# A selective scan with a quantised feed-forward: in slots with sums over states, TensorE does its other jobs first

## The reference, cut to what matters

```python
x = x + ssm(layernorm(x))     # 4 heads of 128 channels, 16 states each
x = x + ffn(layernorm(x))     # inner width 704

# ssm: xz = h @ in_proj.T; x, z = split; x = silu(conv4(x) + b)
#   dt_r, B, C = split(x_proj(x)); delta = softplus(dt_proj(dt_r) + dt_b)
def step(s, inp):                       # for every token, head, channel, state n
    d_t, u_t, B_t, C_t = inp
    s = s * exp(d_t * A[n]) + (d_t * u_t) * B_t[n]
    y_t = sum over n of s[n] * C_t[n]   # the sum over states
    return s, y_t
#   y = (y + x * D) * silu(z); out = y @ out_proj.T

# ffn: fp4(h) = h rounded in blocks of 16 values to the grid 0, .5, 1, 1.5, 2, 3, 4, 6
#   gate, up = fp4(h) @ fp4(w_gate).T, fp4(h) @ fp4(w_up).T
#   out = fp4(silu(gate) * up) @ fp4(w_down).T
```

## Time and profile before

| | |
|---|---|
| time, median of 3 runs | 4897.47 us (4894.6 to 4899.58) |
| the profiled execution: time, span | 4895.54 us, 4893.5 us |
| TensorE matmul busy | 4234.6 us (87%) |
| VectorE busy | 4549.8 us (93%) |
| ScalarE busy | 3509.2 us (72%) |
| POOL busy | 3429.2 us (70%) |
| mean granted TensorE clock | 0.988 of full |
| spreads L904 | 690.1 us, 393.5 us idle before |
| sums L919 (`ybank`, `cross`) | 1003.4 and 1003.1 us, side by side |
| up projection L993 | 357.8 us |
| gate product L797 | 132.5 us, 210.4 us idle before |

### The profile page before, as it was taken

One profiled execution on the slowest core, in us unless ns is written; L12 is line 12 of the kernel. 1 busy time (PEld: TensorE's weight loads), 2 busy tenths in 40 slices (PEclk: granted clock), 3 DMA queues, 4 the chain that ended last, 5 costly groups with the idle time before them and its releaser, 6 DMA issues. The chain is left out here.

```text
span 4893.5 us, 64416 instructions
## 1 busy us (share of the span) xinstructions
PE 4234.6 (87%) x18927; PEld 1986.9 (41%) x19244; DVE 4549.8 (93%) x6828; ACT 3509.2 (72%) x5783; POOL 3429.2 (70%) x2321
## 2 busy tenths in 40 slices
PE   4788888888888888888898888888888888888887
PEld 1234444444444444444444444444444444444434
DVE  6999999999999999999999999999999999999994
ACT  3777777677777777777777777777777777777763
POOL 4777777777776777777777677777777677677763
PEclk8999999999999999999999999999999999999999
DMA  2333333333333333333333333333333333333330
GB/s 89 140 135 123 127 129 125 121 132 126 120 133 124 123 129 129 123 123 134 119 127 131 122 126 127 127 123 130 126 120 133 124 123 129 129 123 123 129 117 19
DMA packets 211138, 600.59 MB, mean 123 GB/s; under 512 B 25446, under 2 KB 76774, under 8 KB 210790
## 3 DMA queue, kind: packets, MB, share of 16 engines
q1 hardware_dynamic: 209088, 594.30, 35.6%
q10 hardware_dynamic: 1702, 2.16, 0.2%
HBM read 575.39 MB, written 20.97 MB: 122 GB/s over the span
## 5 line engine op out<-in xcount | busy, mean ns | idle before, releaser
L629 POOL TENSOR_TENSOR prod<-state,cs 128x1024 f32<-128x1024 f32 x1024 | 2416.5, 2360 | 1320.8 <-DVE state L852 1295.2
L440 ACT ACTIVATE decay<-delta,aneg 128x512 f32<-128x512 f32 x2048 | 1432.6, 717 | 925.3 <-DVE state L852 916.7
L840 DVE TENSOR_TENSOR db<-db,du 128x512 f32<-128x512 f32 x2048 | 1392.0, 680 | 56.7 <-PE db L904 55.5
L852 DVE TENSOR_TENSOR_SCAN state<-decay,carry,db 128x512 f32<-128x512 f32 x1024 | 1292.4, 1262 | 0.0
L852 DVE TENSOR_TENSOR_SCAN state<-decay,db 128x512 f32<-128x512 f32 x1024 | 1232.6, 1204 | 0.0
L904 PE MATMUL db<-pieces,sel 128*128 128x512 bf16 x1798 | 690.1, 386 | 393.5 <-DVE state L852 384.6
L919 PE MATMUL ybank<-prod,ident 64*64 64x512 f32 x4096 | 1003.4, 608 | 28.0 <-DVE hh L790 27.0
L919 PE MATMUL cross<-prod,ident 64*64 64x512 f32 x4096 | 1003.1, 609 | 0.0
L904 PEld LDWEIGHTS db<-pieces,sel 128*128 128x128 bf16 x2048 | 197.8, 97 | 1039.9 <-DVE state L852 809.0
L919 PEld LDWEIGHTS ybank<-prod,ident 64*64 64x64 f32 x4096 | 255.8, 134 | 455.1 <-issue 417.8
L1040 PE MATMUL bank_a<-wd,ht 128*128 128x256 f32 x1536 | 406.0, 389 | 3.2 <-DVE state L852 2.0
(11 more groups left out here) (124 smaller groups left out, 6399.6 us busy)
## 6 DMA issues: line engine op xcount, KB each, us to landing
cs<-c_rows SPq DMA_DIRECT2D x1024, 512.0 KB, 3.6
xin<-in_hidden SPq DMA_DIRECT2D x128, 128.0 KB, 3.6
xres<-in_hidden SPq DMA_DIRECT2D x128, 128.0 KB, 3.4
out_x<-ot SPq DMA_DIRECT2D x128, 128.0 KB, 3.6
c_rows<-xdbl SPq DMA_DIRECT2D x128, 32.0 KB, 3.6
win<-in_win_t SPq DMA_DIRECT2D x1, 1024.0 KB, 10.6
state<-in_w_gate ACTq DMA_DIRECT2D x1, 704.0 KB
state<-in_w_up ACTq DMA_DIRECT2D x1, 704.0 KB
```

The lines of the kernel that those rows point to most:

```text
L440: act.activation(decay[:, g.val() % RING, :], delta[:, gu % 2, :], ACT.Exp, scale=aneg[:, gu % HEADS, gn:gn + 1]).then_inc(decayed, 1)
L629: pool.tensor_tensor(prod[:, r, :, :], state[:, 2 * p:2 * p + 2, :], cs[:, c, :, :], ALU.mult).then_inc(weighted, 1)
L840: dve.tensor_tensor(t[:, :], t[:, :], du[:, gu % 2, :], ALU.mult).then_inc(db_done, 1)
L852: dve.tensor_tensor_scan(state[:, n, :], decay[:, g.val() % RING, :], db[DB_BANK[g.k % TRIP]][:, :], start, ALU.mult, ALU.add).then_inc(sc ...
```

## The change

In TensorE's `step` the call of `side` moves ahead of the loop over the groups of sums. The spread stays first. In slots without sums nothing changes.

```diff
                 if g.within(STEPS):
                     spread_b(b, g)
+                side(b, u, due)
                 for slot, pairs in SUMS.items():
                     if w := due("scan", slot):
                         sum_up(w, pairs)
-                side(b, u, due)
```

## The result

The changed kernel takes 4950.43 us (median of four runs, 4949.61 to 4951.24), the kernel before 4898.52 us on the same occasions. The ratio is 1.0105, 95% interval 1.0088 to 1.0123: slower, by some 52 us. Forecast were 4943 us and a range of 4917 to 4968.

A forecast was written before the change was run, and what follows sets the result against it. VectorE sets the pace (busy 4549.8 of 4893.5 us), TensorE close behind, two chains nearly tied at L787. 2.88 us a trip over 15.3 trips, +44 us, and some 2 us for the first six units gave 4943 us, range 4917 to 4968.

The forecast's parts named there:

- Slot 0: TensorE's L963 waits for `xdbl` without the sums as cover; VectorE's product late by 0.80 us (units 1-3), 0.44 us (units 5-7).
- Slot 3: L993 goes 1.88 us ahead, but L797 then waits for the SiLU and L787 for L516; slot 3 itself saves 0.08 us.
- unit 0: First unit of a trip: `mid` early, slot 3's spread 0.42 us earlier, with slot 3's 0.08 a gain of 0.50 us.
- the middle of 0.62: Unit 4, slot 0: VectorE's product taken as 0.62 us late, between 0.80 and 0.44; unit loss 0.50 us.
- less up to 0.08: Late units, slot 3: deduction from L516's delay, 0.44 - 0.08 less up to 0.08, giving 0.32 us for units 5 to 7.
- +2 us for the first six units: Units before post jobs exist (from unit 6 on): only slot 0 counts, some 2 us.
- Slot 8: Last third of the down projection (L1040) ahead of pairs 0 and 1: value 0, bounds -0.2 to +0.2 us a unit.
- A: Rival, faster: L787 not tied to TensorE's slot 3, only VectorE's own chain counts; -36 us, 4861 us; chance 0.08.
- D: Rival, naive hope: L797's wait shrinks to the SiLU's limit, no slot 0 delay; -100 us, 4797 us; chance 0.02.
- B: Rival, no change: L963's wait shorter than read, units 1 to 7 lose no more than unit 0's 0.50 us; 4897 us; chance 0.05.
- C: Rival, slower: the new idle piece drops TensorE's clock in one unit of eight; 89 us on top, 5032 us; chance 0.04.

The follow-up runs named there:

- e2: Kernel before the change, with side jobs ahead of the sums in slot 0 alone: 4963.39 us, ratio 1.0141.
- e4: Changed kernel, with ScalarE's slot 15 decay behind the two copies of pbank so that `xdbl` ends earlier: 4883.83 us, ratio 0.9982 to the kernel before.
- e1: Kernel before the change, with side jobs ahead of the sums in slot 3 alone: 4886.22 us, ratio 0.9984.
- e5: Kernel before, with side jobs first in slot 3 alone and ScalarE's third decay of slot 6 moved to slot 7, behind L516: 4819.51 us, ratio 0.9841.
- e3: Kernel before the change, with side jobs ahead of the sums in slot 8 alone: 4898.23 us, ratio 1.0006.
- e9: Kernel before, with slots 3 and 8 turned, L1007 alone ahead of slot 0's sums, first SiLU ahead of centring, L516 behind one decay: 4761.87 us, ratio 0.9729.

## Why the prediction was right

**Slot 0.** Forecast was a chain of 3.06 us from the end of `xdbl` to L840; it is 1366.03 - 1362.92 = 3.11 us. The product is late by 0.82 us in units 1 to 3 (forecast 0.80) and 0.50 us in units 5 to 7 (0.44). That this wait is the cause is shown by e2, which has it alone and loses 69 us, and by e4, which halves it and ends 11 us below the kernel before.

**Slot 3.** L797's wait of 0.73 us, for the SiLU, is as forecast, and the SiLU still ends 2.92 us after scan 2. Slot 3 takes 1371.36 - 1367.97 = 3.39 us, as forecast. L787's 0.84 us was forecast as 0.7 to 0.9. e1 and e5 show that the tie at L787 is real.

**Size.** A trip costs 3.5 us; forecast 2.88. Units 1 to 3 grew by 0.70 us (0.64), unit 4 by 0.63 (0.50), units 5 to 7 by 0.44 (0.32); unit 0 shrank by 0.50 us as forecast. Three terms were mis-sized. In unit 4 the product is 0.70 us late, not the middle of 0.62. The step from the spread to L840 was 0.05 us longer: in e4, where slot 1's spread has its record, it is 0.53 us and not 0.47. And in units 4 to 7 the "less up to 0.08" for TensorE being the later one at slot 3 doesn't exist: in late units its spread follows scan 2 by 0.07 us before the change too.

These 0.6 us a trip are 9 us. The span grew by 54.2 us, where the forecast had 46: 52.2 in the fifteen trips behind the first, 4.7 behind the last scan, and -2.7 up to the end of the first trip. The forecast had +2 us for the first six units and no term for what lies behind the last scan (last section). These two misses, -4.7 and +4.7 us, cancel by luck.

**Slot 8** was priced at nothing, and e3 measures nothing.

**The rivals.** A and D (4861 and 4797 us) fail because L787 is tied to TensorE's slot 3: what they promised is what e5 reaches only with L516 out of the way. B fails in units 1 to 3. C, a clock that falls at the new idle piece, does not happen; this is the window that was shown of before, in the changed kernel:

```profile
1300.00:2400.00 1100.00, 958.91 (x4344) 451.55 (x4420) 1037.65 (x1567) 799.70 (x1326) 783.20 (x533) 1.00 0.37 124
```

The granted clock is 1.00, the level of 2.4 GHz, with an idle piece of 1.31 or 1.11 us in front of L963 in seven units of eight. But this is a rounded mean, and so is the 1.00 of the earlier trace rows. In both kernels the clock falls for a moment in 8 of the 15 trips behind the first, at the border of two trips and, between 600 and 4600 us, nowhere else (last section). There the forecast took it for steady, and it costs both kernels the same. The Trainium skill's rule of small idle pieces between groups of matmuls (TensorE: Matmul & The Clock Gate, "A second HAM failure mode: psum-queue depth-cycling") does not show at the pieces of 0.94 or 1.31 us; the clock does swing here, but behind a longer one.

## What to carry to other kernels

Before a job is moved ahead of others on an in-order engine, ask when its operand is ready, and count the work that stood ahead of it as the cover of that wait: 1.88 us of sums had hidden a wait of 1.31 us for a copy. Where an engine's long wait is cured, look for the next instruction that joins two chains; here L787 took back 77 of 92 us, and moving one decay on ScalarE released 68. Of a bundle of jobs turned together, turn each by itself: slot 0 lost 69 us, slot 3 won 8, slot 8 did nothing, and slot 12 has no job to turn. And a mean clock that is rounded to 1.00 can hide short falls: look at narrow windows before differences of a few us are given a cause.

## What was not expected

Unit 0 of a trip comes in more than one length with the same instructions: before the change 37.5 us in some trips and 38.3 us in others, after it 37.0 and 37.8 to 38.1 us. The difference lies in its first three slots. To the end of scan 2 they take 6.72 us in the short kind and up to 7.8 us in the long one, in both kernels alike. What follows takes the same time in both kinds, and is where the change won its 0.50 us (30.79 to 30.29 us).

The traces tell the two kinds apart. Windows at the start of trips in the kernel before, a long one (unit 0 38.27 us) and a short one (37.51 us), then the stretch behind the last scan of the run; the clock is the third number from the end:

```profile
1534.00:1540.00 6.00, 5.38 (x17) 2.99 (x21) 4.63 (x7) 4.89 (x10) 4.83 (x3) 0.72 0.39 139
1830.00:1836.00 6.00, 5.09 (x29) 2.55 (x29) 4.88 (x9) 4.60 (x9) 4.37 (x3) 1.00 0.43 138
4785.20:4893.40 108.20, 81.22 (x305) 54.23 (x297) 44.89 (x108) 42.64 (x74) 31.58 (x36) 0.91 0.04 14
```

In the long kind the granted clock is at its lower level, 1.2 GHz, for part of the window, and the matmuls there are slower. TensorE's rows of the two starts:

```profile
1534.62 0.38 PE L904 MATMUL db<-pieces,sel 128*128 128x512 bf16 x1 [2.64 <-DVE state L852]
...
1535.35 1.92 PE L1069 MATMUL pbank<-uu,xws 128*128 128x512 f32 x2
```

```profile
1830.15 0.38 PE L904 MATMUL db<-pieces,sel 128*128 128x512 bf16 x1 [2.64 <-DVE state L852]
...
1830.80 1.02 PE L1069 MATMUL pbank<-uu,xws 128*128 128x512 f32 x2
```

In all eleven traces the first three slots take 6.72 us where the clock stays up, and 6.87 to 8.53 us where it falls. It falls behind TensorE's wait for a scan in slot 14 of unit 7, 2.64 us before the change and 2.82 after it, the longest of a trip. That wait stands there in every trip, so why the clock falls in some and not in others stays open.

The changed kernel behind its last scan:

```profile
4834.70:4947.60 112.90, 86.44 (x310) 57.44 (x299) 44.93 (x108) 42.41 (x73) 31.28 (x35) 0.83 0.04 13
```

It takes 4.7 us longer there, with a lower mean clock, 0.83 against 0.91, and TensorE busy 5.2 us longer. That goes with the clock and not with the order of the jobs: e3, whose units are as before, takes 112.7 us there at 0.83, and e9 108.1 us at 0.87.

Differences of 5 to 10 us between runs can come from this alone. In e5 the clock falls in all fifteen trips, which costs it 12.6 us against 4.4 in e1: the sum of what the first three slots take above 6.72 us. That is 8 of the 10 us by which e5 misses its number.
